# Audio tower on one core: the pair estimate computed with the tanh tile streamed in column groups and carried back to query rows through memory

## The reference, cut to what matters

```python
scores = jnp.einsum('bqe,bke->bqk', Q, K) / jnp.sqrt(jnp.float32(embed_dim))
hq = jnp.einsum('bqe,he->bqh', Q, W1q)
hk = jnp.einsum('bke,he->bkh', K, W1k)
hid = jnp.tanh(hq[:, :, None, :] + hk[:, None, :, :] + b1)
est = jnp.einsum('bqkh,h->bqk', hid, W2[0]) + b2[0]
attn = jax.nn.softmax(scores + est, axis=-1)
return jnp.einsum('bqk,bke->bqe', attn, V)
```

## Time and profile before

| what | value |
|---|---|
| median of 3 runs | 944.35 us (941.47 to 949.42) |
| profiled execution, whole time | 942.42 us |
| profiled execution, span on the engines | 940.6 us |
| PE busy in the span | 805.5 us (86%) |
| DVE busy | 674.3 us (72%) |
| ACT busy | 485.4 us (52%) |
| POOL busy | 551.1 us (59%) |
| mean granted clock of TensorE | 0.909 |

### The profile page before, as it was taken

One profiled execution on the slowest core, in us unless ns is written; L12 is line 12 of the kernel. 1 busy time (PEld: TensorE's weight loads), 2 busy tenths in 40 slices (PEclk: granted clock), 3 DMA queues, 4 the chain that ended last, 5 costly groups with the idle time before them and its releaser, 6 DMA issues.

```text
span 940.6 us, 21816 instructions
## 1 busy us (share of the span) xinstructions
PE 805.5 (86%) x7926; PEld 505.4 (54%) x7926; DVE 674.3 (72%) x1750; ACT 485.4 (52%) x647; POOL 551.1 (59%) x586
## 2 busy tenths in 40 slices
PE   1125788999999997999899997999899999999885
PEld 0013474756565654656465564656465565756552
DVE  5136668878797966879767977968777968768642
ACT  0037364656474743647464664646475655654422
POOL 1777777777576766737675676747575675710000
PEclk9557888898999988899899998998999989899998
DMA  5788545436272735426262535436251524200000
GB/s 146 185 214 180 99 136 109 123 52 189 38 160 74 153 85 115 116 20 193 43 169 61 124 107 106 128 29 189 39 123 45 110 53 97 64 26 2 9 5 14
DMA packets 79766, 92.41 MB, mean 98 GB/s; under 512 B 30236, under 2 KB 67940, under 8 KB 79660
## 3 DMA queue, kind: packets, MB, share of 16 engines
q1 hardware_dynamic: 60364, 52.88, 21.6%
q0 software_dynamic: 18432, 37.79, 20.2%
q10 hardware_dynamic: 864, 0.30, 0.1%
HBM read 87.62 MB, written 3.28 MB: 97 GB/s over the span
## 4 chain that ended last, share of the span: by engine, by line
PE 52%; DVE 25%; issue 11%; ACT 6%; SPq 3%; DMA 1%; DVEq 0%; ACTq 0%
PE bank L734 10%; PE bank L773 7%; PE bank L883 7%; PE bank L906 6%; PE bank L841 5%; SPq L276 3%; PE bank L808 3%; ACT HT L382 3%; DVE XT L500 2%; PE bank L894 2%; PE bank L855 2%; PE bank L802 2%; PE bank L822 2%; PE bank L794 1%; PE bank L787 1%
## 5 line engine op out<-in xcount | busy, mean ns | idle before, releaser
L351 POOL DMA_INDIRECT G<-in_x,idx x576 | 549.2, 953 | 277.1 <-issue 172.0
L382 ACT ACTIVATE HT<-PXB,c_lneg 128x736 f32<-128x736 f32 x192 | 159.8, 897 | 38.7 <-DMA PXB<-pw 33.2
L883 PE MATMUL bank<-Z,c_w1e 128*128 128x376 f32 x288 | 134.3, 550 | 22.1 <-issue 12.5
L773 PE MATMUL bank<-HT,XN 128*32 128x184 f32 x3072 | 147.3, 344 | 6.5 <-ACT HT L389 5.2
L773 PEld LDWEIGHTS bank<-HT,XN 128*32 128x32 f32 x3072 | 99.2, 118 | 61.9 <-issue 32.8
L389 ACT ACTIVATE HT<-HT 128x2208 f32<-128x2208 f32 x64 | 130.5, 2040 | 0.7
L906 PE MATMUL bank<-GE,c_w2e 128*128 128x376 f32 x256 | 107.1, 524 | 0.0
L452 ACT ACTIVATE HE<-bank,c_fb 128x376 f32<-128x376 f32 x128 | 72.4, 565 | 58.3 <-PE bank L883 57.0
L734 PE MATMUL bank<-VT,c_wdef 128*128 128x380 f32 x256 | 90.5, 509 | 8.1 <-DVE VT L580 8.1
L690 DVE TENSOR_TENSOR GE<-HE,bank 128x376 f32<-128x376 f32 x128 | 68.4, 534 | 31.4 <-PE bank L894 26.4
L883 PEld LDWEIGHTS bank<-Z,c_w1e 128*128 128x128 f32 x288 | 49.5, 203 | 49.2 <-issue 20.3
(11 more groups left out here) (130 smaller groups left out, 994.5 us busy)
## 6 DMA issues: line engine op xcount, KB each, us to landing
xt<-in_x SPq DMA_DIRECT2D x256, 96.0 KB
PXB<-pw SPq DMA_DIRECT2D x16, 768.0 KB
G<-in_x,idx POOLq DMA_INDIRECT x576
XN<-in_x SPq DMA_DIRECT2D x16, 384.0 KB, 6.6
WYB<-pw SPq DMA_DIRECT2D x64, 48.0 KB
out<-OUTS SPq DMA_DIRECT2D x16, 188.0 KB
pw<-nw SPq DMA_DIRECT2D x48, 2.0 KB
pw<-offs SPq DMA_DIRECT2D x48, 2.0 KB
```

The source lines that it names most:

```text
L351: pool.indirect_dma_start(out=G[h][:, col, :], out_offset=None, in_=x.rearrange("b (l c) -> (b l) c", c=C), in_offset=bass.IndirectOffsetO ...
L382: act.activation(HT[half][:, c, :, :].rearrange("p g (w n) -> p g w n", n=4), PXB[h][:, :].rearrange("p (g w i n) -> p i g w n", g=NG, i=2 ...
L773: mm = pe.matmul(bank[0][32 * g:32 * g + 32, HW * c:HW * c + HW], XN[h][:, b, C * ch + 32 * c:C * ch + 32 * c + 32], HT[half][:, k, g, :], ...
L883: pe.matmul(cols(2), w1e[:, e, :], Z2[h][:, :], start=True, stop=True).then_inc(up_full, 1)
```

## The change

The roles of the two operands of the estimate are exchanged, and its result then stands in another place than the scores. The steps:

- `TH` is laid out `[128, q, k]`, and its halves are cut by queries (24 and 23) in place of keys.
- `w2blk` is 128 x 32 (8 columns used) and is the weight. PE pieces `m51` and `m52` stream six queries (282 columns) of `TH` in one matmul; the four matmuls of a half go to the four 32-partition groups of bank 7 (first half) and bank 5 (second half). The 47 matmuls with 47 weight loads of each unit are gone.
- The result has the sequence on the partitions and (q, k) along the columns. ACT copies each bank to `EST`, which lies over `SQ` and `HC`. SP writes each half to a scratch `est` in memory with four DMAs (`e0`, `e1`), waits until they have landed, and reads it back with the queries on the partitions, one DMA a half, into `SC` (`e2`, `e3`).
- DVE `m6` waits for both reads, adds scores and estimate, takes the maximum and negates it. ACT `m6` takes the exponentials in 8 instructions, one a sequence, with the negated maximum as the bias and with the sum as a second output. DVE `m7` has no sum left.
- The order lists are new. SP's is `e0 e2 e1 e3 d9 y0 x0 p0 q0`.

```diff
-KH = 24
+QG = 6
+QH = 4 * QG
...
-    "tensor": ("fs m0 n0 f0 m1 f1 n1 gc f2 ds g0 f3 m2 g1 f4 m3 g2 d0 m4 n2 g3 f5 m5 g4 d1 f6 g5 n3 d2 d3 g6 m7 d4 m8 f7 b3 "
-               "m9 g7 m10 d5 a3 d6 d7 d8 m11 a4 d9 m12").split(),
-    "scalar": ("fs m0 f0 k0 f1 gc f2 f3 k1 m3 f4 m4 m5 k2 k3 f5 h0 m6 m7 f6 h1 f7 h2 m9 h3 a3 d9 m12").split(),
-    "vector": ("m1 g0 n0 m2 g1 m3 m4 g2 c0 g3 c1 g4 m6 g5 m7 n1 c2 m8 g6 b3 g7 m10 t0 t1 d8 m11 a4 m12 t2 m13 t3 m14").split(),
-    "sync": ("x0 p0 y0 q0 d9").split(),
+    "tensor": ("fs m0 n0 f0 m1 f1 n1 gc f2 g0 f3 m2 g1 f4 m3 ds m4 f5 m5 m51 m52 g2 d0 f6 g3 n2 d1 n3 g4 f7 d2 g5 d3 d4 g6 "
+               "m7 m8 d5 b3 m9 g7 m10 a3 d6 d7 d8 m11 a4 d9 m12").split(),
+    "scalar": ("fs m0 f0 k0 f1 gc f2 f3 k1 f4 m3 m4 m5 f5 m51 m52 k2 k3 f6 m6 m7 h0 f7 h1 m9 h2 a3 d9 h3 m12").split(),
+    "vector": ("m1 g0 n0 m2 g1 m3 m4 c0 g2 c1 g3 m6 n1 g4 g5 m7 c2 m8 g6 b3 g7 m10 t0 d8 t1 m11 t2 m12 a4 t3 m13 m14").split(),
+    "sync": ("e0 e2 e1 e3 d9 y0 x0 p0 q0").split(),
...
+            def write_estimate(a):
+                def piece(m, h):
+                    u = 2 * m + h
+                    sp.wait_ge(est_ready, 2 * u + a + 1)
+                    dst = est[bass.ds(u, 1)].rearrange("a b q k -> (a b) (q k)")
+                    for j in range(4):
+                        q0 = QH * a + QG * j
+                        n = min(QG, S - q0) * S
+                        sp.dma_start(dst[:, q0 * S:q0 * S + n], EST[32 * j:32 * j + NB, a, 0:n]).then_inc(est_out[a], 16)
+                return piece
+
+            def read_estimate(a):
+                def piece(m, h):
+                    u = 2 * m + h
+                    q0, q1 = (0, QH) if a == 0 else (QH, S)
+                    src = est[bass.ds(u, 1), :, q0:q1, :].rearrange("a b q k -> q (a b) k")
+                    sp.wait_ge(est_out[a], 4 * 16 * (u + 1))
+                    sp.dma_start(SC[q0:q1, :, 0:S], src).then_inc(est_in, 16)
+                return piece
...
+            def estimates(a):
+                def piece(m, h):
+                    act.wait_ge(est_full, 2 * (2 * m + h) + a + 1)
+                    act.activation(EST[:, a, :], bank[7 - 2 * a][:, 0:QG * S], ACT.Copy).then_inc(est_ready, 1)
+                return piece
+
             def m6(m, h):
                 act.wait_ge(sc_ready, 2 * m + h + 1)
-                act.activation(SC[:, :, :], SC[:, :, :], ACT.Exp).then_inc(exp_ready, 1)
+                for b in range(NB):
+                    ins = act.activation(SC[:, b, 0:S], SC[:, b, 0:S], ACT.Exp, bias=smx[:, b:b + 1],
+                                         accum_out=ssum[:, b:b + 1])
+                ins.then_inc(exp_ready, 1)
...
-                chain(dve.reduce_max(smx[:, :], sc, AX.X))
-                chain(dve.tensor_scalar(smx[:, :], smx[:, :], cs["b2col"][0:S, 0:1], None, ALU.add))
-                dve.scalar_tensor_tensor(SC[:, :, :], sc, cs["b2col"][0:S, 0:1],
-                                         smx[:, :].unsqueeze(2).broadcast_to([S, NB, S]), ALU.add,
-                                         ALU.subtract).then_inc(sc_ready, 1)
+                dve.wait_ge(est_in, 2 * 16 * (2 * m + h + 1))
+                chain(dve.scalar_tensor_tensor(SC[:, :, 0:S], sc, cs["b2col"][0:S, 0:1], SC[:, :, 0:S], ALU.add, ALU.add))
+                chain(dve.reduce_max(smx[:, :], SC[:, :, 0:S], AX.X))
+                dve.tensor_scalar(smx[:, :], smx[:, :], -1.0, None, ALU.mult).then_inc(sc_ready, 1)
...
-                chain(dve.reduce_sum(ssum[:, :], SC[:, :, :], AX.X))
...
-                for k in range(S):
-                    if k in (0, KH):
-                        pe.wait_ge(th_ready, 2 * u + (1 if k == 0 else 2))
-                    mm = pe.matmul(bank[6][0:S, k:k + S * (NB - 1) + 1:S], TH[:, k, :], w2blk[:, :],
-                                   start=False, stop=True, skip_group_check=True)
                 mm.then_inc(s_full, 1)
+
+            def estimate(a):
+                def piece(m, h):
+                    u = 2 * m + h
+                    pe.wait_ge(th_ready, 2 * u + a + 1)
+                    if a == 0:
+                        pe.wait_ge(y_ready, u + 1)
+                    for j in range(4):
+                        q0 = QH * a + QG * j
+                        n = min(QG, S - q0)
+                        mm = pe.matmul(bank[7 - 2 * a][32 * j:32 * j + 32, 0:n * S], w2blk[:, :], TH[:, q0:q0 + n, :],
+                                       start=True, stop=True, skip_group_check=True)
+                    mm.then_inc(est_full, 1)
+                return piece
```

More of the change, by code:

```diff
@@ L90, in end, with audio_tower @@
         self.base, self.n = self.outer + trips * per, 0
-def audio_tower(nc, x, consts, rows, pw, out):
+def audio_tower(nc, x, consts, rows, pw, est, out):
     fp32, bf16, i32 = mybir.dt.float32, mybir.dt.bfloat16, mybir.dt.int32
@@ L124, in audio_tower @@
         w1pad = sb("w1pad", [128, 2, 2, 32])
-        w2blk = sb("w2blk", [128, NB])
+        w2blk = sb("w2blk", [128, 32])
         pe_b = sb("pe_b", [128, S])
@@ L148, in audio_tower @@
         h0 = [sb(f"h0{p}", [128, NB, S]) for p in range(2)]
-        SQ = sb("SQ", [128, COLS])
-        HC = sb("HC", [128, COLS])
+        SQHC = sb("SQHC", [128, 2 * COLS])
+        SQ, HC = SQHC[:, 0:COLS], SQHC[:, COLS:2 * COLS]
+        EST = SQHC[:, 0:2 * QG * S].rearrange("p (a n) -> p a n", a=2)
         Z = sb("Z", [128, NB, S])
@@ L202, in audio_tower @@
         ident_in, first_in = sem("ident_in"), sem("first_in")
+        est_full, est_ready, est_in = sem("est_full"), sem("est_ready"), sem("est_in")
+        est_out = [sem(f"est_out{a}") for a in range(2)]
         x_in = [[sem(f"x_in{p}{j}") for j in range(BP)] for p in range(2)]
@@ L318, in _ @@
             load_x(0, 1)
-            pieces = {"x0": next_x, "p0": write_positions, "q0": spread_positions, "y0": load_rows, "d9": store}
+            pieces = {"x0": next_x, "p0": write_positions, "q0": spread_positions, "y0": load_rows, "d9": store,
+                      "e0": write_estimate(0), "e1": write_estimate(1), "e2": read_estimate(0), "e3": read_estimate(1)}
             early("sync", pieces, -3)
@@ L406, in hidden_tanh @@
                 act.wait_ge(add_ready, 2 * u + half + 1)
-                k0, k1 = (0, KH) if half == 0 else (KH, S)
-                act.activation(TH[:, k0:k1, :], TH[:, k0:k1, :], ACT.Tanh).then_inc(th_ready, 1)
+                q0, q1 = (0, QH) if half == 0 else (QH, S)
+                act.activation(TH[:, q0:q1, :], TH[:, q0:q1, :], ACT.Tanh).then_inc(th_ready, 1)
             def m3(m, h):
@@ L466, in _ @@
             act.wait_ge(lneg_in, 16)
-            pieces = {"m0": squares(0), "m3": m3, "m4": m4, "m5": m5, "m6": m6, "m7": m7, "m9": squares(1), "m12": m12,
+            pieces = {"m0": squares(0), "m3": m3, "m4": m4, "m5": m5, "m51": estimates(0), "m52": estimates(1), "m6": m6, "m7": m7, "m9": squares(1), "m12": m12,
                       "gc": gc, "fs": shared_hidden, "d9": d9, "a3": offsets_out}
@@ L614, in pair_sums @@
             def pair_sums(half):
-                k0, k1 = (0, KH) if half == 0 else (KH, S)
-                dve.tensor_tensor(TH[:, k0:k1, :], hq[:, :].unsqueeze(1).broadcast_to([128, k1 - k0, S]),
-                                  bank[5][:, S + k0:S + k1].unsqueeze(2).broadcast_to([128, k1 - k0, S]), ALU.add).then_inc(add_ready, 1)
+                q0, q1 = (0, QH) if half == 0 else (QH, S)
+                dve.tensor_tensor(TH[:, q0:q1, :], hq[:, q0:q1].unsqueeze(2).broadcast_to([128, q1 - q0, S]),
+                                  bank[5][:, S:2 * S].unsqueeze(1).broadcast_to([128, q1 - q0, S]), ALU.add).then_inc(add_ready, 1)
             def m4(m, h):
@@ L834, in m5 @@
                 for b in range(NB):
-                    mm = pe.matmul(bank[6][0:S, S * b:S * b + S], Y[:, b, :], Z[:, b, :], start=(b == 0), stop=True,
-                              skip_group_check=True)
-                for k in range(S):
-                    if k in (0, KH):
-                        pe.wait_ge(th_ready, 2 * u + (1 if k == 0 else 2))
-                    mm = pe.matmul(bank[6][0:S, k:k + S * (NB - 1) + 1:S], TH[:, k, :], w2blk[:, :],
-                                   start=False, stop=True, skip_group_check=True)
-                mm.then_inc(s_full, 1)
+                    mm = pe.matmul(bank[6][0:S, S * b:S * b + S], Y[:, b, :], Z[:, b, 0:S], start=True, stop=True)
+                mm.then_inc(s_full, 1)
+            def estimate(a):
[11 more added lines that the diff above has]
+                return piece
             def m7(m, h):
@@ L917, in d9 @@
                 mm.then_inc(out_full, 1)
-            pieces = {"m0": centered(0), "m1": variance(0), "m2": spread_rstd(0), "m3": m3, "m4": m4, "m5": m5, "m7": m7,
+            pieces = {"m0": centered(0), "m1": variance(0), "m2": spread_rstd(0), "m3": m3, "m4": m4, "m5": m5, "m51": estimate(0), "m52": estimate(1), "m7": m7,
```

(3 more changed lines are left out.)

4 lines of the change are left out of this document (2 added, 2 removed).

## The result

| what | before | after |
|---|---|---|
| median | 946.88 us (4 runs, 941.47 to 950.22) | 1131.81 us (4 runs, 1125.87 to 1139.24) |
| ratio | 1 | 1.196, 95% interval 1.187 to 1.206 |
| span of the profiled execution | 940.6 us | 1137.4 us |
| mean granted clock of TensorE | 0.909 | 0.834 |
| from one start of DVE `m6` to the next, steps 2 to 11 | 53.0 us on average | 67.3 us on average |

The change makes the kernel 20% slower. The forecast was 1206 us, with a range of 1095 to 1275. Its mechanism is there: the trip of the estimate through memory, begun late by SP. The loss that it forecast is 40% too large (262 us in place of 185), and one step of the argument, on what the trip hides behind, was wrong.

The account below looks back on a forecast made before the run. PE was taken to set nearly the pace before, then SP's queue and the trip: 30.5 + 17 + 25.5 = 73 us a step with loads, 726 for steps 2 to 11, 1206 us in all; range 1095 to 1275.

Parts of the forecast that it names:

- SP's block, 30.5 us from E to e0: From E (ACT has copied the finished unit to OUTS), SP's store, loads, position writes and spread reads take 30.5 us.
- The estimate is ready at E + 20 to E + 25, so SP is 5 to 10 us late: Second tanh ends at E + 19.7 or E + 25.2, copies follow directly; SP reaches its first write 5 to 10 us late.
- The trip, 17 us: Estimate through memory before m6: issues 4.4, two waits 6.6, two read issues 0.9, last landing 5; low 9.3, high about 24.
- The sentence of the prediction on a fixed part of about 2.0 us: Quoted skill on DMA cost: with 2.0 us for each of three landings, the trip is 11.3 us and the time 1116.
- From m6 to E, 25.5 us, of it 2.5 for the clock: Softmax start to step end: 23.0 us of work plus 2.5 for PE's lower clock after idling (bounds 0 and 4.5).
- Sum: Whole kernel: 73 us for each step whose block holds the loads, steps 2 to 11 together 726; in all 1206 us.
- Parts on PE: Estimate on PE: 4.28 us a unit removed, 1.1 added; gain 3.2 a unit, 51 in all where PE sets the pace.
- the cover of 6.7 us: PE's other work before g5 lets it cover a delay of m6 of 6.7 us from the end of m52.
- the rival "the trip is hidden": PE's 9.5 us of other work cover the trip, 3.2 to 3.5 us a unit gained, 888 us; chance 0.05.
- Net: nothing that shows: ACT and DVE: eight exponentials of 0.229, 1.85 us in all, covered by DVE's other work until 0.29 us each.
- The first rival, 1126,: Only the trip counts, SP is free when the estimate is ready; each of 16 steps loses 11.5 us; chance 0.12.
- The signs: Expected in the new profile: gapless SP issues, m6 waits of 15 us and more, idle PE before g5, steps of 70 and more.

Follow-up runs that it names:

- d4: Changed kernel without the estimate's round trip, gathers left out after the first two units: 953.42 us, 1.011 times the kernel before with its gathers.
- d3: Changed kernel with SP's 16 loads ahead of the store, gathers left out after the first two units: 1045.52 us, 1.106 times the kernel before.
- b2: Kernel before with only the softmax of the change (eight exponentials with bias and sum): 1687.39 us on the slow chip, ratio 1.016.
- d2: Changed kernel with the gathers left out after the first two units: 1064.14 us, 1.131 times the kernel before with its gathers.
- c1: Changed kernel with SP's 16 loads ahead of the store, gathers kept: 1765.87 us on the slow chip, 1.061 times the kernel before.
- c3: c1 with both halves of the estimate 24 queries high, the second read 24 rows in place of 23: 1724.24 us on the slow chip, ratio 1.039.
- d1: Kernel before with the gathers left out after the first two units: 937.00 us, 0.993 times the kernel before with them.

## Why the prediction was right, and where it was not

- **SP's block, 30.5 us from E to e0.** Right: 30.4 in the step shown, 29.3 on average over steps 2 to 11. Its terms partly offset each other: loads 13.3 in place of 17, rows 3.0 in place of 0.5.
- **The estimate is ready at E + 20 to E + 25, so SP is 5 to 10 us late.** Too early by about 2 us: the copy of the first half ends at E + 22.9 to E + 25.9, on average at E + 24.6 (498.5 is E + 24.5 in the step shown). It ends 1.1 us behind the second tanh, which the prediction put at nothing, and the tanh itself ends at E + 23.4 on average in place of 21.8 (in d4, without any trip and without gathers, at E + 22.6). SP was late by 1.5 to 7.2 us in these steps, 47 us in all.
- **The trip, 17 us.** Mis-sized, the largest error of the sum: 10.6 us in the step shown, 11.9 on average. The issues of four writes took 1.7 each (2.2 taken). The waits behind them took 1.4 and 1.2 in the step shown, which is a short one, and 2.7 and 1.4 on average (3.3 taken). The last landing took 4.0 with its issue (5.5 taken). I had taken the waits nearest to the position writes, which have 128 pieces of 16 bytes each; the estimate's writes have 8 of 1128 bytes. The small load, 2.0 us, was the better neighbour: the two waits together are 4.1 on average, and in d3, without gathers, each is 1.0 us in nearly every step. The sentence of the prediction on a fixed part of about 2.0 us names a section of the Trainium skill (DMA: Bandwidth & Descriptors, Anatomy of one DMA) whose figure is for DMAs issued by GpSimd, while these are issued by SP; the time that it gives, 1116, came nearer than mine.
- **From m6 to E, 25.5 us, of it 2.5 for the clock.** Right: 26.9 in the step shown, 26.1 on average. At 0.50 the two expert matmuls take 2.71 in place of 1.53, `m8` 3.65 in place of 1.88; `b3` takes 6.66 in place of 5.37.
- **Sum.** A step that holds the loads took 67.3 us in place of 73, and 5.1 of the difference are the trip. Steps 2 to 11 took 673 us in place of 726, the first `m6` came at 128.7 in place of 134.6, steps 1 and 12 to 15 took 283 in place of 299, and the end from the last `m6` 52.3 in place of 44.4. There, until about 1117, the experts' full-width matmuls take 1.62 us in place of 0.90; I had allowed only 2.5 us for that.
- **Parts on PE.** The size was right, 1.15 us against 1.1, and so was the overlap of the column groups. What failed is the step "a gain where PE sets the pace" and, with it, the cover of 6.7 us counted from PE's remaining pieces. The row of VectorE next to the estimate decided. In the kernel before, its two additions into `TH` end at 486.6, and the work that follows brings it to `m6` at 496.7 without a pause:

```profile
484.09 2.52 DVE L616 TENSOR_TENSOR TH<-hq,bank 128x1128 f32<-128x1128 f32 x2
```

  So VectorE had 10 us of its own work there (not 13, as I wrote for d4), and that is what covers tanh, estimate and a part of the trip. That also means that the rival "the trip is hidden" could never have given 888; d4 shows that even no trip at all gives a loss of 16 us.
- **The exponentials.** Their size was wrong: an exponential with a sum takes 0.32 us from start to start, where I took 0.229; 2.6 us in all against 1.85. The reading of the sum starts before the exponential's row ends, and how much it adds is not separated. "Net: nothing that shows" fails in the order of the kernel before, where they cost 26 us (b2). In the changed order the cover I named held: VectorE waited 0.45 us for them in the step shown and 7.0 us in all 16 units. That from 0.29 us each on it would not hold was too strict.
- **The first rival, 1126,** lies nearer to the result than my forecast, and I had given it 0.12. It is not what happened, since SP was behind the copy in all of steps 2 to 11; but it is nearer in kind too, since SP's order was worth only 19 of the 111 us between d4 and d2, and the trip the rest. The range took in both, so the time alone does not tell them apart. How much SP's order is worth with gathers was not measured on an undisturbed chip; the lateness of 47 us bounds it from the trace.
- **The signs.** SP's issues from the store to e0, the idle PE before g5, the clock of 0.50 behind it and the 1.1 us of the estimate are there. VectorE's wait for the reads was forecast at 15 us and more in steps 2 to 11 and is 6.6 to 13.3 us, 10.3 on average; steps of 70 us and more were forecast, and they took 62 to 69 from E to E.

## What to carry to other kernels

Before a faster operation is credited with a gain, look at the row of the engine that consumes its result: if that engine arrives later than the result with no idle time before it, a faster result brings it nothing, and only the time freed on the first engine can help. Here that time came back as idle time. A round trip through memory costs its issues, two landings and a place in an in-order queue, so read from the trace what stands ahead of it there, and try a row count with a large divisor up to 16: 24 rows in place of 23 halved the landing here.

## What the runs showed of the hardware

- One row more in a read, 24 in place of 23, took the time from its issue to the sum that waited for it from 4.0 to 1.8 us, with the same kind of pieces (c1, c3).
- An exponential of 47 x 47 with a sum is two instructions, 0.32 and 0.19 us, and the exponentials start every 0.32 us.
- Four small writes to memory of 8 rows of 1128 bytes were waited for 1.0 us behind the issue of the last in nearly every step without gathers (d3), and 1.0 to 4.2 us with them.
- With 3.1 us a unit less work on PE (d4 against d1), PE idled 5.5 us a step in place of 3.2, and `b3` ran at a granted clock of 0.71 to 0.83 in place of 1.00, 6.4 to 7.4 us in place of 5.4.
- On one of two chips PE, ACT and VectorE stood still for up to 50 us in the steps with gathers, and 16 load issues took 49 us in place of 17. The same kernel took 1661 us there and 943 on the other.
